# Three graph-convolution layers: 19 dense node tiles in place of 17 in layers 1 and 2, and group slots placed as two float32r parts

## The reference

```python
src, dst, norm = _gcn_norm(edge_index, n)          # norm = dinv[src] * dinv[dst]
h = conv(x, W1, b1); h = conv(h, W2, b2); h = conv(h, W3, b3)
# conv: xw = x @ W; out = segment_sum(xw[src] * norm[:, None], dst, n) + b
x = _layernorm(x + h)
```

## Time and profile before

| | |
|---|---|
| Runs, median | 2393.74 us |
| Profiled execution, time | 2390.54 us |
| its span in the profile | 2388.7 us |
| granted TensorE clock, mean | 0.941 of 2.4 GHz |
| POOL busy | 1663.6 us (70%) |
| PE busy | 2012.8 us (84%) |
| DVE busy | 1358.8 us (57%) |
| ACT busy | 754.5 us (32%) |
| HBM traffic | 247 GB/s over the span |

### The profile page before, as it was taken

One profiled execution on the slowest core, in us unless ns is written; L12 is line 12 of the kernel. 1 busy time (PEld: TensorE's weight loads), 2 busy tenths in 40 slices (PEclk: granted clock), 3 DMA queues, 4 the chain that ended last, 5 costly groups with the idle time before them and its releaser, 6 DMA issues.

```text
span 2388.7 us, 31641 instructions
## 1 busy us (share of the span) xinstructions
PE 2012.8 (84%) x9902; PEld 1092.5 (46%) x9902; DVE 1358.8 (57%) x3393; ACT 754.5 (32%) x1445; POOL 1663.6 (70%) x1746
## 2 busy tenths in 40 slices
PE   6665778999889987888899898997799999999863
PEld 6321224444444432345555555554455655555421
DVE  8425765666666653254444444445555666555677
ACT  0602543444344432232223222223322223222211
POOL 0257777777777777477777777777577777777772
PEclk9867989999999999999999999999899999999986
DMA  7556887888888888578888888889788888888894
GB/s 276 216 166 189 269 276 228 248 246 248 254 272 274 256 247 249 167 223 242 241 236 251 243 253 261 265 263 306 204 246 254 254 249 259 271 277 280 275 309 156
DMA packets 283058, 591.28 MB, mean 248 GB/s; under 512 B 72467, under 2 KB 125648, under 8 KB 282896
## 3 DMA queue, kind: packets, MB, share of 16 engines
q0 software_dynamic: 136624, 446.62, 61.9%
q1 hardware_dynamic: 146272, 142.67, 18.0%
HBM read 523.67 MB, written 65.45 MB: 247 GB/s over the span
## 4 chain that ended last, share of the span: by engine, by line
POOL 30%; issue 10%; PE 8%; DMA 7%; DVE 2%; DVEq 0%; ACT 0%; ACTq 0%; POOLq 0%
POOL ring L969 30%; DMA ring<-y_dram,kept 5%; PE ps L1295 4%; PE ps L1183 2%; DMA out_dram<-row_sb 2%; PE ps L1194 1%; DVE row_sb L1972 0%; PE ps L1348 0%; DVE acc L1903 0%; DVE ln L1958 0%; DVE h_sb L1949 0%; DVE h_sb L1956 0%; DVEq L1899 0%; DMA y_dram<-acc 0%; DVE acc L2100 0%
## 5 line engine op out<-in xcount | busy, mean ns | idle before, releaser
L969 POOL DMA_INDIRECT ring<-y_dram,kept x1698 | 1635.1, 963 | 581.3 <-issue 503.4
L1183 PE MATMUL ps<-ring,onehot 128*32 128x512 f32 x3396 | 479.3, 631 | 165.0 <-DMA ring<-y_dram,kept 163.6
L2100 DVE SCALAR_TENSOR_TENSOR acc<-ps,acc 128x512 f32<-128x512 f32 x442 | 304.9, 690 | 301.9 <-PE ps L1295 289.5
L1295 PE MATMUL ps<-dense_first,wide_a 128*128 128x512 f32 x1020 | 296.5, 413 | 13.5 <-DVE dense_first L2071 6.4
L1876 DVE TENSOR_TENSOR onehot<-ps,kept 128x128 f32<-128x128 f32 x429 | 122.8, 287 | 249.8 <-PE ps L1183 248.5
L1903 DVE SCALAR_TENSOR_TENSOR acc<-ps,mask,acc 128x512 f32 x288 | 202.8, 746 | 78.8 <-issue 73.0
L1295 PEld LDWEIGHTS ps<-dense_first,wide_a 128*128 128x128 f32 x1020 | 190.5, 193 | 117.8 <-issue 53.4
L1295 PE MATMUL ps<-dense_next,wide_a 128*128 128x512 f32 x730 | 221.3, 412 | 10.5 <-ACT wide_a L1536 10.5
L1183 PEld LDWEIGHTS ps<-ring,onehot 128*32 128x32 f32 x3396 | 73.5, 109 | 338.4 <-issue 332.4
L1295 PE MATMUL ps<-dense_first,y_rows 128*128 128x512 f32 x680 | 203.8, 422 | 0.6
L1194 PE MATMUL ps<-onehot 128*128 128x512 f32 (+1 forms) x288 | 172.0, 681 | 28.8 <-issue 14.3
(11 more groups left out here) (286 smaller groups left out, 2128.9 us busy)
## 6 DMA issues: line engine op xcount, KB each, us to landing
ring<-y_dram,kept POOLq DMA_INDIRECT x1698, 4.8
onehot<-a_dram SPq DMA_DIRECT2D x408, 64.0 KB
y_dram<-acc SPq DMA_DIRECT2D x99, 256.0 KB, 9.9
a_dram<-ring SPq DMA_DIRECT2D x17, 784.0 KB, 5.6
acc<-in_x_dram SPq DMA_DIRECT2D x1, 12288.0 KB
y_dram<-acc SPq DMA_DIRECT2D x12, 1024.0 KB, 10.8
out_dram<-row_sb SPq DMA_DIRECT2D x48, 256.0 KB
w_sb<-in_x_dram SPq DMA_DIRECT2D x24, 256.0 KB
```

The source lines that it names most:

```text
L969: pool.indirect_dma_start(ring[:, s, :], None, y_dram[layer], bass.IndirectOffsetOnAxis(ap=rows, axis=0)).then_inc(done, 16)
L1183: mm = pe.matmul(ps[k * WIDE:(k + 1) * WIDE, g % BANKS, :], wide_hot[:, r, k, :], ring[:, r * CPQ + k, :], start=opens, stop=closes, tile_ ...
L1295: mm = pe.matmul(ps[:, bank, :], wide_slots[n % WIDE_SLOTS][:, P * k:P * (k + 1)], y_parts[(TILES * (layer - 1) + tile) % YSLOTS][:, part, :],
L2100: dve.scalar_tensor_tensor(out=rows, in0=ps[:, UNIT_BANKS[n % len(UNIT_BANKS)], :], scalar=0.5, in1=rows, op0=ALU.mult, op1=ALU.add).then_ ...
```

## The change

DENSE is 19 and FIRST_SOURCE 20. So layers 1 and 2 have 24 dense groups, 125 quads, 494 gathers and 247 units each, where they had 22 groups, 131 quads, 518 gathers and 221 units. Layer 0 has 662 gathers as before and 247 windows in place of 221; the 26 new ones stand where up to now each quad had one, so that some quads have two. The source tiles that must be read back from memory in a layer are 20 in place of 16.

A group's slots are no longer placed by one fp32 matmul. ACT copies them to float32r (`slots_high`), DVE subtracts that copy from the sums in PSUM (`split_slots`, `slots_low`), and PE places both by two float32r matmuls into one bank. Each part has one buffer, so ACT's copy waits for the placing of the group before. PE's placing, and its opening of a bank that an earlier group used, now wait for DVE's split. DVE does the split at the end of the quad that closes the group.

In layer 0, a quad that has units and two windows builds the second window behind the first unit and not behind all, and ACT keeps it ahead of the widening for the next quad.

```diff
--- before.py
+++ after.py
@@ -23,7 +23,7 @@
 CPG = CPW * CPQ
 RING_QUADS = 5
 STORE_QUADS = 7
-DENSE = 17
+DENSE = 19
 DENSE_SPARE = 700
 EARLY_DENSE = 8
 PAIR = 2
@@ -31,7 +31,7 @@
 A0_SLOTS = 4
 WIDE0_SLOTS = 2
 BOUNDARY = 3
-FIRST_SOURCE = 16
+FIRST_SOURCE = 20
 BLOCK = 4
 YSLOTS = 8
 ASLOTS = 5
@@ -332,7 +332,9 @@
         y_words = 2 * D
         wide0 = sb("wide0", [P, WIDE0_SLOTS, PAIR * P], F32R)
         y0_rows = sb("y0_rows", [P, 4, D], F32R)
-        sb("below_dense", [P, STORE_QUADS * CPQ * P - y_words], F32)
+        sb("below_slots", [P, RING_QUADS * CPQ * WIDE], F32)
+        place_rows = sb("place_rows", [P, 2 * P + 2 * D], F32R)
+        sb("below_dense", [P, STORE_QUADS * CPQ * P - RING_QUADS * CPQ * WIDE - 2 * P - 2 * D - y_words], F32)
         dense_last = sb("dense_last", [P, y_words], F32R)
         sb("ring_rows", [P, RING_QUADS * CPQ, D], F32)
         dense_first = sb("dense_first", [P, (RING - RING_QUADS * CPQ) * D], F32R)
@@ -414,11 +416,11 @@
         assert LINE + FAR <= b_at
         hots_at = RING_QUADS * CPQ * WIDE
         wide_hot = small[:, 0:hots_at].rearrange("p (q c n) -> p q c n", q=RING_QUADS, c=CPQ)
-        place_hot = small[:, hots_at:hots_at + 2 * P].rearrange("p (b n) -> p b n", b=2)
+        place_hot = place_rows[:, 0:2 * P].rearrange("p (b n) -> p b n", b=2)
         slots_at = hots_at + 2 * P
         slot_place = lo_f[:, CHUNKS:CHUNKS + GROUPS]
         assert CHUNKS + GROUPS <= COLS
-        slots = small[:, slots_at:slots_at + 2 * D].rearrange("p (b d) -> p b d", b=2)
+        slots_high, slots_low = place_rows[:, 2 * P:2 * P + D], place_rows[:, 2 * P + D:2 * P + 2 * D]
         spare_at = slots_at + 2 * D
         spare = small[:, spare_at:STORE_QUADS * CPQ * P]
         extra = ring[:, RING_QUADS * CPQ:RING, :].rearrange("p c d -> p (c d)")
@@ -560,6 +562,7 @@
         slots_ready = sem("slots_ready")
         summed = sem("summed")
         slots_copied = sem("slots_copied")
+        slots_split = sem("slots_split")
         place_ready = sem("place_ready")
         placed = sem("placed")
         added = sem("added")
@@ -1174,7 +1177,7 @@
                 opens, closes = a == 0, n + 1 == QUADS_TO[g]
                 pe.wait_ge(hot_ready, n + 1)
                 if opens and g >= BANKS:
-                    pe.wait_ge(slots_copied, g - BANKS + 1)
+                    pe.wait_ge(slots_split, g - BANKS + 1)
                 if not closes_layer(n):
                     pe.wait_ge(gathered[r], landed(n))
                 for k in range(len(chunks_of(n))):
@@ -1188,11 +1191,12 @@
                 own = own_of(g)
                 rows = LAST_ROWS if own == GROUPS - 1 else P
                 pe.wait_ge(place_ready, g + 1)
-                pe.wait_ge(slots_copied, g + 1)
+                pe.wait_ge(slots_split, g + 1)
                 if g > 0:
                     pe.wait_ge(added, 2 * g)
-                pe.matmul(ps[:, PLACE_BANK, :], place_hot[0:rows, g % 2, :], slots[0:rows, g % 2, :],
-                          start=True, stop=True).then_inc(placed, 1)
+                pe.matmul(ps[:, PLACE_BANK, :], place_hot[0:rows, g % 2, :], slots_high[0:rows, :], start=True, stop=False)
+                pe.matmul(ps[:, PLACE_BANK, :], place_hot[0:rows, g % 2, :], slots_low[0:rows, :],
+                          start=False, stop=True).then_inc(placed, 1)
 
             def turn_done_tile(t):
                 turn = TURN_OF[0][t]
@@ -1325,10 +1329,12 @@
                     for t in finished_at(0, q):
                         multiply_tile(TURN_OF[0][t], TURN_BANK)
                     build(q)
-                    for u in units:
+                    for u in units[:1]:
                         dense0_unit(u)
                     for w in windows[1 if units else 2:]:
                         build_window(w)
+                    for u in units[1:]:
+                        dense0_unit(u)
 
             def last_tiles(layer):
                 place_group(GROUP_AT[layer + 1] - 1)
@@ -1480,9 +1486,9 @@
             def copy_slots(g):
                 rows = LAST_ROWS if own_of(g) == GROUPS - 1 else P
                 act.wait_ge(summed, QUADS_TO[g])
-                if g >= 2:
-                    act.wait_ge(placed, g - 1)
-                act.copy(slots[0:rows, g % 2, :], ps[0:rows, g % BANKS, :]).then_inc(slots_copied, 1)
+                if g >= 1:
+                    act.wait_ge(placed, g)
+                act.copy(slots_high[0:rows, :], ps[0:rows, g % BANKS, :]).then_inc(slots_copied, 1)
 
             def keep_windows(windows):
                 for w in windows:
@@ -1576,9 +1582,12 @@
                         keep_turned(TURN_OF[0][t])
                     for k in splits0_at(q):
                         high0(k)
+                    if units:
+                        keep_windows(windows[1:])
                     for u in units0_at(q + 1):
                         widen_a0(u)
-                    keep_windows(windows[1 if units else 2:])
+                    if not units:
+                        keep_windows(windows[2:])
                     for t in finished_at(0, q):
                         scale_rows(0, t, h_sb, TURN_OF[0][t])
 
@@ -1886,6 +1895,12 @@
                 dve.wait_ge(summed, n + 1)
                 if n + RING_QUADS < ALL_QUADS:
                     stage_places(n + RING_QUADS)
+
+            def split_slots(g):
+                rows = LAST_ROWS if own_of(g) == GROUPS - 1 else P
+                dve.wait_ge(slots_copied, g + 1)
+                dve.tensor_tensor(slots_low[0:rows, :], ps[0:rows, g % BANKS, :], slots_high[0:rows, :].bitcast(F32),
+                                  ALU.subtract).then_inc(slots_split, 1)
 
             def add_group(g, units=0):
                 dve.wait_ge(placed, g + 1)
@@ -2133,6 +2148,8 @@
                                 finish_norm(TURN_OF[layer][t])
                     for tile in splits_at(layer, q):
                         low_part(layer, tile)
+                    if n + 1 == QUADS_TO[g]:
+                        split_slots(g)
                 if layer == LAYERS - 1:
                     for t in finished_at(layer, DENSE_QUADS - 1)[-1:]:
                         finish_norm(TURN_OF[layer][t])
@@ -2152,6 +2169,8 @@
                     for u in units0_at(q)[:-2]:
                         add0_unit(u, g)
                     build(q)
+                    if q + 1 == QUADS_TO[g]:
+                        split_slots(g)
                     for k in splits0_at(q):
                         low0(k)
 

```

## The result

The changed kernel takes 2348.49 us (median of 4 runs, 2344.56 to 2349.53), the kernel before on the same chip 2391.54 (2386.71 to 2395.39). The ratio is 0.983, with a 95% interval of 0.981 to 0.9851. Forecast were 2362 us, and a range of 2342 to 2382. The profiled execution took 2344.56 us, with a span of 2342.7 in place of 2388.7: 46.0 us less.

A forecast was written before the change was run, and what follows sets the result against it. POOL's gathers were taken to set all three layers' pace, PE close behind, stores the end. From 2390.5 us: -30.3 layer 1, -17.9 layer 2, +9.8 tiles, +6 splits, +3 small terms = 2361; forecast 2362, range 2342 to 2382.

The forecast's parts named there:

- rival 2: PE limits layer 1 too, or the last stretch keeps 5.15 us per store with whole splits: 2380 us, chance 0.17.
- Layer 2 up to quad 102: PE becomes the bound there; quad 102 summed 543 us into the layer, gaining 17.9 us instead of 30.6.
- PE's price list: PE's costs from layer 2's trace: 1.22 us per quad, 1.82 per unit, 0.87 per fp32 placing; 0.46 taken for the new placing.
- I add 6: Layer 2 up to quad 102: 6 us added to PE's list, after 12 us unexplained in the kernel before.
- rival 1: Layer 2 keeps the gathers' pace, quad 102 at 530 us: 2349 us, or 2333 with extra tiles hidden; chance 0.20.
- The ring: Gather slots between POOL and PE: PE may be 15 us late before POOL notices.
- The split in the loop: DVE's 0.68 us subtraction ends its quad, placing follows some 3 us later, so PE does not wait in the loop.
- Rival 3: The split comes too late in the loop and holds PE's next units; at a 1.0 us stall 2400 us, chance 0.08.
- the prediction's own sign of being wrong: Wrong if PE waits for DVE's split ahead of L1197, layer 1 exceeds 630 us, or POOL slows in layer 0.
- Rival 4: The two float32r placing matmuls cost 0.87 us like the fp32 one; layer 2 pays 13.5 us: 2375 us, chance 0.05.
- The last stretch: Layer 2's final row stores, 25 instead of 23: +9.8 us for two more tiles, +6 for seven splits.
- Layer 0, block 0 and the ends: Three small terms, +1 us each: layer 0's 26 more windows, block 0's extra units in layer 2, splits at layer ends.

The follow-up runs named there:

- e1: Changed kernel with 19 dense tiles, but each group placed by one fp32 matmul as before, without the split: 2360.4 us, ratio 0.9864.
- e3: Changed kernel with each group's split subtraction done twice on DVE: 2357.71 us, ratio 0.9844.
- e4: Changed kernel with layer 2's finished rows normalized in place and stored from two buffers in turn, not through `row_sb`: 2344.76 us, ratio 0.9799.
- e5: Changed kernel with one of eight matmuls left out of each full unit in layer 2's loop, on a second, slower chip: 2735.41 us, ratio 0.9878.
- e11: The kernel of e5 (changed kernel, one matmul fewer per full unit in layer 2's loop) again, on a third, slow chip: 2701.01 us, ratio 0.9856.
- e2: Changed kernel with 17 dense tiles as before, keeping the split and the two float32r placings: 2399.21 us, ratio 1.0031.
- e12: The kernel before, unedited, run on the third, slow chip for its stages: 2740.1 us, ratio 0.9998.

## Why the prediction was right, by its own steps

**Layer 1: right.** -32.7 us against -30.3. 24 gathers at the old pace of 1.2605 are 30.3. The other 2.4 are the pace itself, 1.2556 in place of 1.2605. I count that as luck: e1, e3 and e4 have 1.2643, 1.2634 and 1.2626 in the same stage, each in one execution. PE at 96% kept up; rival 2 (PE limits layer 1 too) does not hold here, with 13.1 us of waits for gathers left and POOL waiting for PE for 2.1 us in all. In e1, without PE's cheaper placings, PE still waits for gathers for 2.7 us, and POOL for PE for 0.3.

**Layer 2 up to quad 102: the mechanism right, the size 6 us off.** PE's price list gave 522 us behind a first sum at +15. The first sum came at +14.8 (1669.27 - 1654.46), and the quad at 536.8: 522.0 us of PE. The list hit. What failed is the term "I add 6". The 12 us of the kernel before that the list left unexplained are the price of the lower clock: from 1700.05 to 2247.58 its granted clock stood at the lower level, 1.2 GHz, for 23.8 us, which costs half of that, 11.9. In the changed kernel it stood at 2.4 GHz from 1669.27 to 2191.24 without a break, and nothing is left unexplained. So the gain here was 23.8 and not 17.9, between the forecast and the 530 us of rival 1, which PE never reached. The 522.0 are no accident of one execution: from the first sum to quad 102, e3 (1680.51 to 2202.49) and e4 (1673.34 to 2195.32) need 521.98 us each, whatever POOL and DVE did. e1 shows the price list at work a second time (13.6 us for 13.5): a stretch whose time follows PE's work to 0.2 us is set by neither the ring nor the tables' transfers. The direct test from the other side, a lighter PE (e5, e11), has not been run where gathers are 1.25 us apart.

The rule that was weighed, 131 ns per 512-column matmul (the Trainium skill, "TensorE: Matmul & The Clock Gate", section "Back-to-back issue gap"), is contradicted once more: PE at 1.00 and 499 of 500 us busy still takes 1.82 us for a unit's eight, 228 ns each.

**The ring: right, and nearly used up.** PE needs 522.0 us for 102 quads, POOL 102 x 4 x 1.255 = 512; PE falls 10 us behind, and the ring takes it: POOL waits only 0.6 us for PE from 1700 to 2200, and 21.3 us behind 2200, when dense tiles are being finished and it no longer matters.

**The split in the loop: right where PE is the bound, not everywhere.** Rival 3 is refuted where it would have cost something: PE never waits for the split in layer 2 up to quad 102, and e3 doubles it there and quad 102 does not move. But "in the loop PE does not wait" was too much. PE did stand ahead of L1197 for DVE's split: 5.1 us in layer 1's last quads, and in layer 0 14 times for up to 1 us (and once for 15.0, at the first group). That was the prediction's own sign of being wrong. It cost nothing that shows: POOL waited for PE in layer 1 for 2.1 us in all, and layer 0 is 1.1 us shorter than before.

**The placing's price: right.** 0.46 us, as taken. Rival 4 (the two matmuls cost 0.87) falls.

**The last stretch: 4 us too dear.** +11.9 against +15.8. Two more tiles cost 6.4 (e1) and not 9.8: 3.2 each. The 4.9 that I took came from means over the whole stretch, waits and intervals with a group beside them included; that an added tile has none of these is the likely reason, and not shown. The splits cost 5.5 (changed against e1) or 8.0 (e2 against before), 6 had been taken, and the way was as forecast: each of the seven placings started as soon as the split was done.

**Layer 0, block 0 and the ends: too small to matter, here.** -1.1, and +1.6 at the second boundary, against +3 in all. On the third chip layer 0 is 14 to 28 us longer in the three kernels that have the 26 more windows than in e12, and there the term is not small. With one execution of before, and three of the same layer that differ by 13.8 among themselves, the size is uncertain.

Over all, the sum missed by 16.6 us (-29.4 against -46.0): 2.4 of luck in POOL's pace, 5.9 in layer 2, 3.9 in the last stretch, and 4.4 in edges each costed at +1 or at nothing. All four err to the same side, so the gain that was forecast is two thirds of the one that came.

## What to carry to other kernels

When two engines are within a few per cent of each other, write the price list of the second, unit by unit, and believe it: here a stretch in which it no longer waited had no unexplained rest, since that rest was the lower clock, which went with its pauses. And where a view gives no releaser for a wait ("issue", "remote"), look which instruction of the other engines ended just before, and whose semaphore it was. A buffer between them turns a rate that is too slow into a time at which it starts to matter, and a layer that ends before that loses nothing. An edit that makes one engine cheaper at the cost of another pays only where the first is the bound: the split alone lost 6 us, and won 12 beside the 19 tiles.

## What the runs showed that I had not expected

- Chips differ by 15% on this kernel (2393, 2743 and 2768 us), with gathers, matmuls and DVE operations of the same length in the profile, and the gain of the change differs with them: 0.983 on one, 0.989 on another. The last stretch is as long on both; the loops, in which four engines hand each other small pieces, are longer, and there the other engines wait for semaphores of PE.
- POOL's pace almost without waits differs between kernels that have the same code for it, 1.2556 to 1.2643 us: 3.5 to 4.3 us in a layer of 494 gathers. Each is one execution, so it is not known whether the kernel or the execution makes it.
- PE's granted clock in layer 2 rose from 0.98 to 1.00 when its pauses went, so that filling them with work also gave back the 12 us that the lower clock had cost.
